# Giving out scattered rows' places by group of four tiles, with the shared experts written out among the routing steps

## The reference

```
logits = flat @ router_w                       # n = 2048 rows, 64 experts
scores = softmax(logits)
topk_idx = top_k(logits + router_bias, 4)
topk_scores = scores[topk_idx] / sum           # 4 gates per row
g = silu(flat @ wg[e]); u = flat @ wu[e]       # hidden width 64
routed = sum over the 4 experts of gate * ((g * u) @ wd[e])
shared = sum over 2 shared experts of (silu(flat @ swg) * (flat @ swu)) @ swd    # hidden width 256 each
out = routed + shared
```

## Time and profile before

| what | us |
|---|---|
| median of 3 runs | 1237.13 |
| the profiled execution's own time | 1233.89 |
| its span, first to last instruction | 1232.1 |
| mean granted TensorE clock | 0.862 |

### The profile page before, as it was taken

The page is one execution under the profiler, slowest core; times in us unless marked ns, Lnnn a source line. Parts: engine busy times, 40 slices in busy tenths (PEclk is TensorE's granted clock), DMA queues, the critical chain, the costliest instruction groups (busy, mean ns, idle before and its releaser), DMA issues.

```text
span 1232.1 us, 23970 instructions
## 1 busy us (share of the span) xinstructions
PE 924.1 (75%) x7700; PEld 705.7 (57%) x7700; DVE 701.2 (57%) x1839; ACT 448.6 (36%) x955; POOL 505.2 (41%) x566
## 2 busy tenths in 40 slices
PE   3985899976399988895557599996759997889000
PEld 2764677746288766683445345545648876777000
DVE  4777777735945433353467689943975543445333
ACT  2552555542011244452233168871201144455000
POOL 3000422216477422233785343214377632232676
PEclk9997999986699998998677679997679998999555
DMA  6284899949842489873387367705242359995343
GB/s 228 56 171 81 167 218 217 258 103 243 185 141 102 140 254 267 256 242 119 100 190 193 64 98 108 104 1 144 61 138 102 123 181 238 274 273 186 120 131 115
DMA packets 159010, 196.99 MB, mean 160 GB/s; under 512 B 17328, under 2 KB 137648, under 8 KB 155824
## 3 DMA queue, kind: packets, MB, share of 16 engines
q1 hardware_dynamic: 99744, 94.56, 35.4%
q0 software_dynamic: 22848, 68.18, 17.2%
q10 hardware_dynamic: 36304, 32.84, 9.1%
HBM read 132.86 MB, written 90.18 MB: 181 GB/s over the span
## 4 chain that ended last, share of the span: by engine, by line
PE 24%; DVE 8%; DMA 6%; POOL 5%; issue 3%; SPq 2%; ACT 2%; ACTq 2%; DVEq 0%; POOLq 0%
PE ps L783 4%; POOL big L522 4%; PE ps L823 4%; PE ps L633 3%; DMA yd<-tmp 3%; PE ps L602 3%; DMA big<-yd,slot 2%; PE ps L618 2%; PE ps L794 2%; PE ps L835 2%; PE ps L806 1%; ACTq L310 1%; PE ps L710 1%; SPq L342 1%; SPq L350 1%
## 5 line engine op out<-in xcount | busy, mean ns | idle before, releaser
L853 ACT ACTIVATE tmp<-ps 128x256 f32<-128x256 f32 (+1 forms) x328 | 145.3, 472 | 125.5 <-PE ps L806 32.0
L940 ACT ACTIVATE tmp<-ps 128x384 f32<-128x384 f32 (+1 forms) x256 | 135.7, 544 | 72.4 <-PE ps L621 46.5
L480 POOL DMA_INDIRECT xd<-big,slot x128 | 126.4, 987 | 83.3 <-DVE slot L1334 44.9
L522 POOL DMA_INDIRECT big<-yd,slot x128 | 131.1, 1024 | 42.0 <-issue 25.5
L448 POOL COPY arena<-negmax 24x2048 bf16<-24x2048 bf16 x32 | 60.6, 1893 | 175.7 <-ACT negmax L853 175.7
L602 PE MATMUL ps<-arena 96*128 96x256 bf16 (+1 forms) x512 | 105.8, 278 | 13.2 <-DVEq L285 10.6
L618 PE MATMUL ps<-arena 120*128 120x256 bf16 (+1 forms) x512 | 100.8, 264 | 0.9 <-POOL arena L448 0.3
L1391 DVE SCALAR_TENSOR_TENSOR tmp<-tmp,ps 128x128 f32<-128x128 f32 x128 | 36.8, 287 | 104.0 <-ACT tmp L1009 103.3
L1078 DVE SCALAR_TENSOR_TENSOR X<-big,comb,X 128x256 f32<-128x256 f32 (+1 forms) x128 | 57.9, 481 | 66.7 <-DMA big<-yd,slot 66.7
L1401 DVE COPY tmp<-ps 128x256 f32<-128x256 f32 x128 | 53.7, 424 | 68.6 <-PE ps L835 37.5
L1184 DVE TENSOR_REDUCE tmp<-ps 128x2 f32<-128x512 f32 x128 | 81.6, 683 | 7.8 <-PE ps L602 7.8
(11 more groups left out here) (168 smaller groups left out, 1917.4 us busy)
## 6 DMA issues: line engine op xcount, KB each, us to landing
big<-xd POOLq DMA_DIRECT2D x128, 256.0 KB, 4.7
arena<-parts SPq DMA_DIRECT2D x192, 128.0 KB, 5.6
xd<-zero SPq DMA_DIRECT2D x8, 2048.0 KB, 14.1
spill<-in_we SPq DMA_DIRECT2D x128, 128.0 KB, 3.2
yd<-tmp POOLq DMA_DIRECT2D x64, 256.0 KB, 3.2
yd<-tmp ACTq DMA_DIRECT2D x64, 256.0 KB, 3.5
parts<-arena SPq DMA_DIRECT2D x128, 96.0 KB
arena<-in_we SPq DMA_DIRECT2D x8, 1024.0 KB, 9.2
```

Source lines behind the costliest of these rows:

```text
L480: pool.indirect_dma_start(xd[:, :], bass.IndirectOffsetOnAxis(ap=slot[:, i, k:k + 1], axis=0), xn_all[:, i, :], None).then_inc(scattered.s ...
L522: pool.indirect_dma_start(gring[n % GRING], None, yd[:, :], bass.IndirectOffsetOnAxis(ap=slot[:, b * TB + m % TB, m // TB:m // TB + 1], ax ...
L853: return act.activation(dst, src, ACT.Copy)
L940: act.activation(prob[h % 8][:, 0:n], ps[2 + h % 2][:, 0:n], ACT.Exp).then_inc(exp_ready.sem, 1)
```

## The change

It gives out places per group, as soon as that group's ranks are there. An overflow tile is now given out in the group in which an expert first needs it, so overflow tiles are ordered by group and then by expert: `old_at` says where rows of an expert go that fit in tiles given out so far, `limit` up to which rank, `new_at` where the later ones go. `tiles` and `ends` carry the number of overflow tiles and their running sum from one group to the next. PE's extra product in `ranks` gives the counts up to and with this group, and the ranks are read from PSUM by DVE, without ACT's copy. DVE normalises the first four tiles, POOL the other twelve. The shared experts' steps are written out without a loop, among the routing steps. PSUM banks are dealt out anew: all transposes use ps[7], all logits ps[5], ranks and counts ps[6].

```diff
 POOL
-                for i in range(NT):
-                    if i == 0 or i == TB:
-                        pool.wait_ge(*rstd_ready(r, 2 * (2 - r) - 1 + (i > 0)))
+                pool.wait_ge(*rstd_ready(r, 2 * (2 - r)))
+                for i in range(GT, NT):
                     pool.tensor_scalar(xn_all[:, i, :], X[:, i, :], mv[:, i, 0:1], rstd[:, i:i + 1],
-                                       ALU.subtract, ALU.mult).then_inc(rn_ready.sem, 1)
+                                       ALU.subtract, ALU.mult).then_inc(rp_ready.sem, 1)
...
+                pool.wait_ge(*rp_ready(r, NT - GT))
 PE
+                    pe.wait_ge(*xnt_ready(r, b))
...
-                        mm = pe.matmul(at, onesb, cum[g % 2], start=False, stop=True)
-                    mm.then_inc(rank_done.sem, 1)
+                        pe.matmul(at, onesb, cum[g % 2], start=False, stop=True)
+                    pe.matmul(ps[6][:, GT * E:GT * E + E], onesb, cum[(g + 1) % 2], start=True, stop=True).then_inc(rank_done.sem, 1)
+                def shared_in(s, half):
+                    pe.wait_ge(*sg_ready(r, max(2 * s - 1 + half, 0)))
+                    pe.wait_ge(*xnt_ready(r, s + 1))
...
+                def shared_out(s):
+                    pe.wait_ge(*sg_ready(r, s * 2 + 2))
+                    pe.wait_ge(*sx_added(r, s))
...
                 turn_normal(0)
                 turn_normal(1)
                 logits(0)
+                turn_normal(2)
+                turn_normal(3)
+                for s in range(B + 1):
+                    if s < B:
+                        shared_in(s, 0)
+                    if s >= 1:
+                        shared_out(s - 1)
+                    if s in (1, 2):
+                        turn_normal(2 * s + 2)
+                        turn_normal(2 * s + 3)
+                    if s < B:
+                        shared_in(s, 1)
+                    if s in (0, 1, 2, 4):
+                        ranks(min(s, 3))
+                    if s < 3:
+                        logits(s + 1)
+                    if s == 5:
                         pe.wait_ge(*tef_ready(r, 1))
+                        pe.transpose(ps[6][0:1, 3 * P:4 * P], tef, ident[:, :]).then_inc(teT_done.sem, 1)
 ACT
+                for b in range(4):
+                    keep_turned(b)
+                exponents(0)
+                for s in range(B):
+                    shared_tanh(s, 0)
+                    if s in (1, 2):
+                        keep_turned(2 * s + 2)
+                        keep_turned(2 * s + 3)
+                    if s in (1, 2, 4):
+                        exponents(min(s, 3))
+                    shared_tanh(s, 1)
 DVE
+                def place(g):
+                    now, was = tiles[g % 2], tiles[(g + 1) % 2]
+                    end = ends[g % 2]
...
+                    dve.wait_ge(*rank_done(r, g + 1))
+                    link(dve.tensor_scalar(cnt_i, ps[6][:, GT * E:GT * E + E], float(P - 1), None, ALU.add))
+                    dve.tensor_tensor(far, rank, over(limit), ALU.is_ge)
+                    link(dve.tensor_single_scalar(cnt_i, cnt_i, 7, ALU.arith_shift_right))
+                    dve.tensor_tensor(slotmap, rank, over(old_at), ALU.add).then_inc(rank_out.sem, 1)
+                    link(dve.tensor_copy(ntf, cnt_i))
+                    link(dve.tensor_scalar(now, ntf, -1.0, 0.0, ALU.add, ALU.max))
+                    link(dve.tensor_tensor(grown, now, was, ALU.subtract))
+                    link(dve.tensor_tensor_scan(end, one64, grown, 0.0 if g == 0 else ends[(g + 1) % 2][:, E - 1:E], ALU.mult, ALU.add))
+                    link(dve.tensor_tensor(new_at, end, now, ALU.subtract))
+                    link(dve.tensor_scalar(new_at, new_at, float(P), float((E - 1) * P), ALU.mult, ALU.add))
+                    link(dve.tensor_tensor(moved, new_at, old_at, ALU.subtract))
+                    link(dve.tensor_tensor(far, far, over(moved), ALU.mult))
+                    dve.wait_ge(*rank_out(r, g + 1))
+                    link(dve.tensor_tensor(slotmap, slotmap, far, ALU.add))
+                    for a in range(GT):
+                        ins = dve.tensor_tensor(prod[...], oh[:, g * GT + a, :, :], slotmap[:, a:a + 1, :]..., ALU.mult)
+                    link(ins)
+                    link(dve.tensor_reduce(slotf, prod..., AX.X, ALU.add))
+                    dve.tensor_copy(slot[:, 4 * g:4 * g + 4, :]..., slotf).then_inc(slot_ready.sem, 1)
+                    link(dve.scalar_tensor_tensor(out=grown, in0=grown, scalar=0.0, in1=moved, op0=ALU.is_gt, op1=ALU.mult))
+                    dve.tensor_scalar(limit, now, float(P), float(P), ALU.mult, ALU.add)
+                    link(dve.tensor_tensor(old_at, old_at, grown, ALU.add))
+                    link(dve.tensor_scalar(cmp, end, jcol[:, 0:1], None, ALU.is_le))
+                    link(dve.tensor_reduce(owner[:, g:g + 1], cmp, AX.X, ALU.add))
...
+                for half in range(2):
+                    dve.wait_ge(*rstd_ready(r, 2 * (2 - r) - 1 + half))
+                    for i in range(half * TB, half * TB + TB):
+                        dve.tensor_scalar(xn_all[:, i, :], X[:, i, :], mv[:, i, 0:1], rstd[:, i:i + 1],
+                                          ALU.subtract, ALU.mult).then_inc(rn_ready.sem, 1)
+                pick(0); shared_gate(0); place(0)
+                pick(1); shared_gate(1); dve.wait_ge(*rp_ready(r, NT - GT)); add_shared(0); place(1)
+                pick(2); shared_gate(2); add_shared(1); place(2)
+                shared_gate(3); add_shared(2); pick(3)
+                shared_gate(4); add_shared(3); place(3); name_tiles()
+                shared_gate(5); add_shared(4); share_tiles(); gates(0); gates(1)
+                shared_gate(6); add_shared(5); gates(2); gates(3); gates(4)
+                shared_gate(7); add_shared(6); gates(5); gates(6); gates(7); add_shared(7)
                 barrier(dve, "dve")
```

More of the change, by code:

```diff
@@ L186, in build @@
         tef = tmp[:, 2048:2049]
+        slotf = tmp[:, 2052:2068]
+        owner = tmp[:, 2068:2072]
+        ends = [tmp[:, 2112:2176], tmp[:, 2176:2240]]
         duo = sb("duo", [1, P])[:, :]
[L188 to L192, removed]
+        slotmap = tmp[:, 4096:4352].rearrange("p (i e) -> p i e", i=GT)
+        far = tmp[:, 4352:4608].rearrange("p (i e) -> p i e", i=GT)
+        old_at, new_at, moved, grown, limit = (tmp[:, 4608 + 64 * k:4672 + 64 * k] for k in range(5))
         sth = tmp[:, 5120:6144]
@@ L756, in _ @@
                 logits(0)
-                for g in range(GROUPS):
-                    if g + 1 < GROUPS:
-                        turn_normal(2 * g + 2)
-                        turn_normal(2 * g + 3)
-                        logits(g + 1)
-                    ranks(g)
-                pe.wait_ge(*cum_ready(r, GROUPS))
-                pe.matmul(ps[4][:, 0:E], onesb, cum[0], start=True, stop=True).then_inc(cnt_done.sem, 1)
-                pe.wait_ge(*xnt_ready(r, B))
-                pe.wait_ge(*ex_ready(r, GROUPS))
@@ L966, in keep_turned @@
                     act.wait_ge(*rT_done(r, b + 1))
[L967 to L974 removed]
+                    copy(xnt_all[:, :, b * S:b * S + S], ps[7][:, :].rearrange("p (c n) -> p c n", c=KC)).then_inc(xnt_ready.sem, 1)
@@ L981, in _ @@
-                    copy(rank[:, g * GT:g * GT + GT, :],
-                         ps[3][:, 0:GT * E].rearrange("p (t e) -> p t e", t=GT)).then_inc(rank_out.sem, 1)
-                def shared_step(s, i, has):
-                    if has[0]:
-                        for half in range(2):
-                            act.wait_ge(*gu_done(r, s * 2 + half + 1))
-                            act.wait_ge(*sg_ready(r, s * 2 + half - 1))
-                            act.activation(sth[:, half * 512:(half + 1) * 512], ps[half][:, :], ACT.Tanh,
-                                           scale=0.5).then_inc(sth_ready.sem, 1)
@@ new lines, in _ @@
+                pick(0)
+                shared_gate(0)
+                place(0)
+                pick(1)
+                shared_gate(1)
+                dve.wait_ge(*rp_ready(r, NT - GT))
+                add_shared(0)
+                place(1)
+                pick(2)
+                shared_gate(2)
+                add_shared(1)
+                place(2)
+                shared_gate(3)
+                add_shared(2)
+                pick(3)
+                shared_gate(4)
+                add_shared(3)
@@ new lines, in _ @@
+                place(3)
+                name_tiles()
+                shared_gate(5)
+                add_shared(4)
+                share_tiles()
+                disp_base[0] += d[0]
+                gates(0)
+                gates(1)
+                shared_gate(6)
+                add_shared(5)
+                gates(2)
+                gates(3)
+                gates(4)
+                shared_gate(7)
+                add_shared(6)
+                gates(5)
+                gates(6)
+                gates(7)
```

200 lines of the change are left out of this document (80 added, 120 removed).

## The result

The changed kernel took **1194.51 us** (median, 1189.84 to 1204.38, 4 runs) against 1237.88 for the kernel before on the same chip (1236.69 to 1243.57, 4 runs): ratio 0.9661, 95% interval 0.9614 to 0.9708. The profiled execution took 1196.16 us, span 1194.6. Two later sets gave 1194.79 against 1236.18 (0.9664, 0.9625 to 0.9703) and 1197.42 against 1235.45 (0.9702, 0.9655 to 0.9749).

What follows compares the result with a forecast made beforehand. Routing was taken as bound by engines taking turns, with PE's idle stretch and late scatters both to move: 20.8 us a stage less 1 and 1.3, net 18.5, 37 in both, giving 1200 us; range 1187 to 1216.

Steps and rivals of the forecast that it cites:

- Start: Routing stage's beginning: DVE normalises tiles 0 to 3, tiles 2 and 3 held by POOL; picking 2.5 us earlier.
- Placing: DVE giving out one group's places: 7.9 us a group, 6.7 of it up to the slots.
- First products: PE's first shared-expert batch: first half 6.9 us at 1.2 GHz, second 3.45; group 0's slots at 308.9.
- Last group's slots: DVE's placing of group 3: slots at 364.3, after 2.7 us of waits for PE.
- my list of what would show it wrong: Granted clock 0.5 to 0.7 between 300 and 345, scatters over 1.35 us apart, late group 3 slots, longer expert stage.
- Scatters: POOL's chain: first scatter at 309.9, 64 in 82.6 us, loads at 394.6; DVE's work costs them nothing.
- held by DVE: Rival, POOL's scatters held for DVE's instructions: loss from a 1.61 us step, 1350 at 2.5; chance 0.03.
- Both chains end together: Routing stage's end: POOL's chain and DVE's last addition end within a microsecond or so of each other.
- Experts: Expert rows start at about 398.5 instead of 419.27, 20.8 us earlier a stage.
- Taken back: Losses per stage: 1 us for PE's clock, 1.3 for the expert stage's lost head start; net 18.5.
- given back: Rival: the expert stage stretches by what routing gains, 1225 to 1237; chance 0.03.
- clock: Rival: PE stays at 1.2 GHz through the first batches, 1225 in all, up to 1229; chance 0.13.

Runs made afterwards that it cites:

- again: Changed kernel repeated without edit: 1194.79 us against 1236.18 for the kernel before; repeated as again_2: 1197.42 against 1235.45.
- run 0: Not a follow-up: first of two routing and expert stages within one execution; routing 143.6 and 145.3 us before, 122.3, 119.2 and 121.4 after.
- run 1: Not a follow-up: second routing and expert stage within the same execution; routing 143.3 us before in both traces, 119.5, 119.8 and 119.5 after.
- places_alone: Places by group, shared experts left behind routing; against kernel before: 1341.17 us, ratio 0.9854; second set 0.9946; places_alone_3, without standstills, 1263.74, 1.0249.
- fewer_scatters: Changed kernel without the last group's 16 scatters: 1260.56 us against 1356.93 for the kernel before, ratio 0.9278, with standstills.
- hold_second: Changed kernel, POOL's first scatter waiting for the second group's slots: 1312.43 us, 0.9659 to kernel before; hold_second_2 1317.97, 0.9657; both with standstills.

## Why the prediction was right

Forecast 1200, range 1187 to 1216; measured 1194.5. By its steps, times into the stage (its 276.43, the trace's 280.53):

- *Start.* Tiles 2 and 3 at 4.6, held by POOL: they ended at 3.5 (283.11 + 0.90), not held. Picking starts at 9.0, not 10.5. I had taken the holding between two bounds with no row that showed it, and the lower was right (279.8 in the forecast's clock, 279.9 measured).
- *Placing.* 7.9 us and 6.7 to the slots: 7.8 and 6.75. The bounds were not needed.
- *First products.* Forecast from 13.2 to 23.5 with the first half at 1.2 GHz; they ran from 11.5 to 20.9 (292.04 to 301.38), as the first half took 5.7 us and not 6.9, the granted clock rising within it (0.50 up to 296, 0.95 after). Slots of groups 0 to 2 were forecast at 32.5, 48.9, 65.4 and came at 29.6, 45.9, 62.3: some 1.6 from the start, 1.0 from the clock. The spacing of 16.4 held (16.3, 16.4).
- *Last group's slots.* 87.9 forecast, 88.4 measured, the lead of 3 us lost: DVE waits 4.37 us for ACT's result at 349.78 after a window at clock 0.57 (333 to 341). Such a clock was on my list of what would show it wrong, but it lasted 8 us and not 45. It was absent in again (1.00 in 330 to 345), where these slots came 4.3 us earlier (84.8 us after the first power, against 89.1).
- *Scatters.* First at 33.5 forecast, 30.6 measured; 82.6 us for 64, measured 83.8; loads at 118.2, measured 116.4. Most steps were 1.26 to 1.27 whether DVE was busy or not, and the mean was 1.31; the rival "held by DVE" needed 1.61 and fell. But my reading that DVE costs the scatters nothing was wrong. Eight of the 64 took 1.08 to 1.93 us and not 0.96, 3.1 us more in all (1.8 in the kernel before). The longest ones lie beside DVE's one-hot comparison, as in these rows of POOL and of DVE:

```profile
330.14 1.93 POOL L478 DMA_INDIRECT xd<-big,slot  x1 [0.30 <-issue]
```
```profile
330.02 1.23 DVE L1280 TENSOR_TENSOR oh<-iotb,tmp 128x1024 bf16<-128x1024 bf16 x1
```

  The scatter ends 0.82 us after the comparison does; another of 1.76, at 313.92, ends 0.83 us after its own. In the three traces of the changed kernel 18 comparisons run beside scatters, and 17 of them lie beside a scatter of 1.26 to 1.95 us. The kernel before did all its comparisons before its first scatter, so the rows that I judged by could not show it. The rule of the Trainium skill, SBUF — State Buffer, "SBUF: two separate sides", thus had a small price here. The page of the Trainium skill limits it, as my forecast did not, to VectorE instructions in a two-port mode, or with two SBUF inputs against a GpSimd instruction that reads SBUF. The trace agrees with the second kind: the comparison has two SBUF inputs, and beside most of DVE's other work a scatter took its 0.96 us. This is read from when they run; no run took the comparison away. POOL never waited at a group's border.
- *Both chains end together.* Confirmed: DVE's last addition ends the stage in run 0 (401.97, rows turned at 402.07), the load in run 1. One sign of "right" failed: PE was idle 2.82 us before its last down product (388.6 to 391.4 in the forecast's clock), where I had allowed 2.
- *Experts.* 122.1 forecast, 121.5 and 118.8 measured. So the term of 20.8 us a stage was undersized: 23.6 over all traces. In run 1 the parts can be followed: the first scatter starts at 29.7 and not 33.5, the scatters take 83.9 and not 82.6, and the first rows are turned 3.2 us after the first load's issue and not 3.9.
- *Taken back.* 2.3 a stage forecast. The expert stages grew by 0.4 and 1.0 us in the mean (151.45 to 151.83, 155.05 to 156.00), inside their own spread; with loads issued less far ahead they did not stretch by the 4 us I would have called wrong. That a head start counts at all is seen only in places_alone_3. Of the 4 to 9 us that the whole lacks, no cause is shown.

The forecast gain of 37 stands against 38 to 43: a routing gain 5.6 larger over both stages, less what other stretches gave back. Rival "given back" would have needed expert stages 12 us longer or more; "clock" would have needed slots at 312. The gain's cause, that idle times of two engines were filled with each other's work, was not only argued: places_alone_3 removes that half and the stage becomes longer than before. The other half, that the early scatters are needed too, rests on the rows (the load is last in four of six stages) and not on a run. Where the whole gain came out at 38, in the set of again_2, its nearness to the forecast 37 is luck: a routing gain forecast 5.6 us too small and a loss elsewhere that was 4.6 in the forecast and 9, of unshown cause, in the runs offset each other.

## What to carry to other kernels

Releasing a DMA chain early gains nothing while another chain ends the stage; count both chains to the same end, and move both. Breaking a serial step into parts pays for its extra instructions only where other work fills the waits between the parts: here the parts alone cost 28 us, and with the filling the same parts gained 38 to 43. Once two chains end within 1 or 2 us of each other, a step that brings one forward must leave the other where it is: 3 us off POOL's chain gave nothing, since the same step set DVE's back.

## What the runs showed of the hardware that I had not expected

In the six traces from two of the five sets, TensorE, VectorE and ScalarE stood still or nearly so for 15 to 48 us at a time, and the sync engine's queue slowed down, while GpSimd issued indirect scatters. The kernel before, untraced there, took 120 us more than its 1237. It is not fixed to a chip: one chip gave 1362.15 in one set and 1235.45 in the next. Windows of places_alone in its first set:

```profile
342.00:350.00 8.00, 0.00 (x0) 0.00 (x0) 0.00 (x0) 0.00 (x0) 3.41 (x4) 0.50 0.22 78
...
420.00:460.00 40.00, 40.00 (x187) 35.20 (x186) 20.79 (x44) 4.78 (x8) 0.00 (x0) 1.00 0.00 0
```

In 342 to 350 PE, DVE and ACT start nothing. POOL issues its scatters on time until 346.32, then waits for slots; DVE's next instruction comes 4.7 us later, at 350.98. After the last scatter PE is busy 40.00 of 40. Where work trickles through, single matmuls come some 2 us apart with no semaphore awaited ("issue"), and DMA issues of the sync engine come 5.6 us apart, where the changed kernel has them 0.6 to 2.0 us apart (375.64 to 389.46). The timelines of PE and of the sync engine's queue, in the same trace:

```profile
387.48 1.24 PE L772 MATMUL ps<-swd,tmp 128*128 128x256 f32 x5
390.66 0.38 PE L772 MATMUL ps<-swd,tmp 128*128 128x256 f32 x1 [1.93 <-issue]
392.76 0.38 PE L772 MATMUL ps<-swd,tmp 128*128 128x256 f32 x1 [1.72 <-issue]
```
```profile
387.12 0.01 SPq L378 DMA_DIRECT2D spill<-in_we  x1
392.72 0.70 SPq L377 DMA_DIRECT2D spill<-in_we  x1
```

Three engines that stop and a queue that slows, without a semaphore, under one engine's scatters, look like instructions that arrive late, but no run here measured the supply of instructions, and what differs between a set with and one without standstills is open. Two facts bear on it: the stage shrank with the number of scatters (152 us with 48, 181 to 198 in kernels with 64), and where the scatters paused, DVE resumed 4.1 to 7.1 us after the last one (places_alone, fewer_scatters, hold_second and hold_second_2). For a measurement it means: a kernel before and after must be timed in the same set. places_alone was 0.5 to 1.5% faster than before with standstills and 2.5% slower without.
